# A graph network kernel: the order of three small things

## What is computed

```
h = max(layernorm(x), 0);  x = x + attention_and_splines(h)
h = max(layernorm(x), 0);  x = x + three_convolutions(h)

attention_and_splines:
  e = leaky_relu(s[row] + t[col]);  ex = exp(e - max over the row's edges)
  agg = sum(ex * h[col]) / sum(ex)                  # per node
  out = silu(agg) @ base_w.T + einsum(cubic B-splines of agg (8 per feature), spline_w)
three_convolutions, l = 0, 1, 2:
  agg = (normalised adjacency with self loops) @ (x @ W[l].T) + b[l]
  x = relu(gamma[l] * batchnorm(agg) + beta[l])
```

## Time and profile before

| what | us |
|---|---|
| median of 3 runs (614.23 to 615.87) | 615.74 |
| the profiled execution | 615.99 |
| its span, first to last instruction | 614.2 |
| PE busy | 588.1 (96%) |
| DVE busy | 435.3 (71%) |
| ACT busy | 338.8 (55%) |
| POOL busy | 36.2 (6%) |

### The profile page before, as it was taken

The page is one execution under the profiler, slowest core; times in us unless marked ns, Lnnn a source line. Parts: engine busy times, 40 slices in busy tenths (PEclk is TensorE's granted clock), DMA queues, the critical chain, the costliest instruction groups (busy, mean ns, idle before and its releaser), DMA issues.

```text
span 614.2 us, 9800 instructions
## 1 busy us (share of the span) xinstructions
PE 588.1 (96%) x3951; PEld 364.3 (59%) x3951; DVE 435.3 (71%) x745; ACT 338.8 (55%) x447; POOL 36.2 (6%) x40
## 2 busy tenths in 40 slices
PE   6798989999999999999999999999999999999994
PEld 2566856565645555555555555687557855587552
DVE  7995999987669999995499779362374335552555
ACT  3897647767799989892798334044132333142112
POOL 1000430000000000000000030041100020000000
PEclk9899799899999999999999999999999999999999
DMA  8980400000410000000000000250200000000112
GB/s 301 316 282 29 189 1 2 1 2 1 162 75 1 0 2 1 1 1 1 0 2 1 0 1 2 68 214 1 68 2 0 1 1 0 2 2 0 43 43 83
DMA packets 11502, 29.18 MB, mean 48 GB/s; under 512 B 735, under 2 KB 2399, under 8 KB 11201
## 3 DMA queue, kind: packets, MB, share of 16 engines
q1 hardware_dynamic: 11456, 28.54, 12.7%
HBM read 22.71 MB, written 5.84 MB: 46 GB/s over the span
## 4 chain that ended last, share of the span: by engine, by line
PE 68%; DVE 2%; ACT 0%; DVEq 0%; issue 0%; ACTq 0%
PE bank L1892 33%; PE bank L1976 21%; PE bank L1933 13%; DVE BHL L1306 1%; PE bank L1876 0%; PE bank L1870 0%; ACT Z L977 0%; DVE lnx L1444 0%; DVE BHL L1312 0%; DVE lnp L1442 0%; DVEq L1443 0%; DVE kx L1274 0%; DVE kh L1295 0%; DVE Z L1547 0%; ACTq L126 0%
## 5 line engine op out<-in xcount | busy, mean ns | idle before, releaser
L1892 PE MATMUL bank<-BHL,WKh 128*128 128x418 f16 x1152 | 204.5, 339 | 1.2 <-DVE BHL L1306 1.2
L1892 PEld LDWEIGHTS bank<-BHL,WKh 128*128 128x128 f16 x1152 | 111.2, 97 | 94.2 <-DVE BHL L1306 1.6
L1976 PE MATMUL bank<-C,YH 128*128 128x418 f16 x360 | 122.4, 340 | 0.0
L1976 PE MATMUL bank<-C,YL 128*128 128x418 f16 x360 | 122.3, 340 | 0.0
L1547 DVE SCALAR_TENSOR_TENSOR Z<-bank,yback,dvb 128x418 f32<-128x418 f32 x36 | 23.4, 651 | 52.1 <-PE bank L1976 52.1
L973 ACT ACTIVATE bnc<-bnm,tiny 128x1 f32<-128x1 f32 x12 | 3.5, 294 | 92.0 <-DVE bnm L1555 92.0
L1976 PEld LDWEIGHTS bank<-C,YH 128*128 128x128 f16 x360 | 35.3, 98 | 28.8 <-issue 0.8
L1976 PEld LDWEIGHTS bank<-C,YL 128*128 128x128 f16 x360 | 35.2, 98 | 28.0
L936 ACT ACTIVATE YH<-bank,dvl 128x512 f16<-128x512 f32 x30 | 20.5, 687 | 56.6 <-PE bank L1933 56.6
L1497 DVE SCALAR_TENSOR_TENSOR YL<-bank,dvl,YH 128x512 f16<-128x512 f32 x30 | 22.0, 749 | 39.1 <-ACT YH L936 39.1
L1933 PE MATMUL bank<-GWH,XH 128*128 128x512 f32 x120 | 47.6, 396 | 0.0
(11 more groups left out here) (246 smaller groups left out, 984.3 us busy)
## 6 DMA issues: line engine op xcount, KB each, us to landing
WKf<-in_wk SPq DMA_DIRECT2D x9, 1024.0 KB, 6.6
c_scratch<-C SPq DMA_DIRECT2D x1, 3200.0 KB, 10.8
C<-c_scratch SPq DMA_DIRECT2D x1, 3200.0 KB, 10.1
GWf<-in_gwT SPq DMA_DIRECT2D x3, 1024.0 KB, 11.1
XT<-in_xT SPq DMA_DIRECT2D x1, 2500.0 KB, 8.8
outT<-Z SPq DMA_DIRECT2D x3, 625.0 KB, 3.0
Wt<-in_WT SPq DMA_DIRECT2D x1, 1024.0 KB, 8.2
hx<-in_x SPq DMA_DIRECT2D x1, 1024.0 KB
```

The source lines that it names most:

```text
L1892: ins = mm(bank[:, 4 * (g % 2) + o, 0:G], lhs, rhs, start=(u == 0 and q == 0 and i == 0), stop=(u == UNITS - 1 and q == PAIR - 1 and i == 2))
L1976: ins = mm(bank[:, u % YB, 0:G], Y[:, j, o * P:(o + 1) * P], C16[:, j, g * G:(g + 1) * G], start=(j == 0 and i == 0), stop=(j == NT - 1 an ...
```

## The change

1. In DVE's attention loop `denominators(0)` moves from n = 14 to n = 13 and `weight_scale` from 13 to 14.
2. In the spline loop turn 0's own last steps (`above`, `turn_low`, `upper`, `lower`) come right behind `spline(0)` on DVE, turn 1 counts as `fresh`, and ACT does `turn_high(0)` two operations earlier, ahead of `middle(2)`.
3. The last chunk is cut into four pieces: first columns 1000 to 1249, then three pieces of 334, 334 and 332. DVE does the first alone, scale and shift in a tensor_scalar, then maximum with 0 and addition of x in one, while ACT does the relu of the others. SP issues four stores in place of three.

```diff
+OWN = 250
+THIRD = (N - OWN + 2) // 3
-PIECES = [...] + [(DC - 1, g * G, min((g + 1) * G, N)) for g in range(NG)]
+PIECES = [(c, 0, N) for c in range(DC - 1)] + [(DC - 1, N - OWN, N)] + [
+    (DC - 1, i * THIRD, min((i + 1) * THIRD, N - OWN)) for i in range(3)]
...
-                if n == 1:
-                    turn_high(0)
                 squares_of(n, i)
...
                     clipped(n + 1)
+                if n == 0:
+                    turn_high(0)
                 if n + 2 < NG * TURNS:
                     middle(n + 2)
...
-                        if k == c:
+                        if k == c and not (last and n1 - n0 == OWN):
                             nc.scalar.activation(Z[:, c, n0:n1], Z[:, c, n0:n1], ACT.Relu, bias=bnc[:, 1, c:c + 1],
                                                  scale=bnc[:, 0, c:c + 1]).then_inc(relu_set, 1)
...
                 if n == 13:
+                    denominators(0)
+                if n == 14:
                     weight_scale()
-                if n == 14:
-                    denominators(0)
...
-                fresh = n in (0, 2 * TURNS)
+                fresh = n in (0, 1, 2 * TURNS)
...
-                elif n:
+                elif n > 1:
                     silu_low(2, 1)
...
                 spline(n, i)
+                if n == 0:
+                    above(0)
+                    turn_low(0)
+                    upper(0)
+                    lower(0)
...
-                            dve.wait_ge(relu_set, l * DC + (i + 1))
+                        if k == c and i == DC - 1:
+                            dve.wait_ge(bn_set, l * DC + (c + 1))
+                            V.tensor_scalar(Z[:, c, n0:n1], Z[:, c, n0:n1], bnc[:, 0, c:c + 1], bnc[:, 1, c:c + 1],
+                                            ALU.mult, ALU.add)
+                            dve.drain()
+                            V.scalar_tensor_tensor(Z[:, c, n0:n1], Z[:, c, n0:n1], 0.0, XT[:, c, n0:n1],
+                                                   ALU.max, ALU.add).then_inc(out_set, 1)
+                        elif k == c:
+                            dve.wait_ge(relu_set, l * DC + (i + 1 if i < DC - 1 else i))
```

More of the change, by code:

```diff
@@ L117 @@
 MEAN_BANKS = (4, 5, 0)
-PIECES = [(c, 0, N) for c in range(DC - 1)] + [(DC - 1, g * G, min((g + 1) * G, N)) for g in range(NG)]
+OWN = 250
+THIRD = (N - OWN + 2) // 3
+PIECES = [(c, 0, N) for c in range(DC - 1)] + [(DC - 1, N - OWN, N)] + [
+    (DC - 1, i * THIRD, min((i + 1) * THIRD, N - OWN)) for i in range(3)]
 VAR_BANKS = (6, 1)
```

## The result

The changed kernel takes 612.92 us (median of 20 runs, 612.68 to 614.53), the kernel before 615.78 (median of 20, 614.16 to 617.51): 2.86 us less. The ratio is 0.996 with a 95% interval of 0.9951 to 0.9969. The profiled execution took 614.23 us, 612.4 of it span.

A forecast was written before the change was run, and what follows sets the result against it. PE was taken as the bound from attention to the last convolution; 2.33 + 0.17 + 0.35 = 2.85 us off the profiled 615.99 gave 613.1, and with the median 0.25 lower, 612.9 us; eight in ten 611.0 to 614.6.

The forecast's parts named there:

- Part A: Attention, group 0: inverting weight sums before the scale removes PE's 2.3 us wait and half clock; gain 2.33 us.
- The four limits: Attention groups 0 to 2: scale hidden, then row copy, second inversion and second row copy cut 4.25 us to 2.33.
- Part B: Splines: finishing turn 0 first moves PE's 1.2 us wait to turn 1, nearly 1 us there; gain 0.17 us.
- Part C: Kernel's end: DVE alone does 250 columns, last addition 0.31 us ahead, store 0.04; gain 0.35 us.
- Stalls that add up: Rival 1: DVE is not the limit, so 4.25 + 1.2 + 0.35 = 5.8 us gained, 609.9 us; chance 0.10.
- Half clock at a new place: Rival 2: one half-clock stretch returns ahead of group 2 or at turn 1, costing 1.6 us, 614.5 us; chance 0.17.
- the slower case: Rival 3: clock falls behind each new wait from 134.5 us on; two give 616.2 us, a third 617.8; chance 0.04.
- Sums too late for DVE: Rival 4: group 0's sums come after DVE's 104.69, or scale late for group 1; gain 1.5 to 2.3; chance 0.07.

The follow-up runs named there:

- both moves above: Changed kernel with the weight split behind the second inversion and row copy, and ACT's rounding right behind the squares; 610.87 us, 0.9914 of the kernel before.
- the first part alone: Kernel before with only group 0's weight sums inverted at tile 13 and the scale at tile 14; 613.48 us, ratio 0.9958.

## Why the prediction was right, point by point

**Part A: mechanism right, size 0.3 us too small, by one assumption: that DVE's total work up to the row copy is unchanged.** The four limits came in the order forecast: scale hidden, row copy, second inversion, second row copy. Forecast was 2.33 us, measured 2.65. The difference is DVE's scale: in the earlier trace rows it takes 1.82 us from 104.69 to 106.51, with a pause of 0.44 us in it that the trace lays to issue:

```profile
105.98 0.15 DVE L1236 TENSOR_SCALAR wsi<-wsi 128x1 int32<-128x1 int32 x1 [0.44 <-issue]
```

In the changed kernel its steps follow each other every 0.23 us (108.85, 109.08) and it takes 1.44. From the inversion to the row copy DVE now needs 110.96 - 106.06 = 4.90 us (its first instruction starts 0.19 ahead of the 106.25 above) where I had 109.97 - 104.69 = 5.28. Of these 0.38 us PE got 0.34: it started group 2 at 135.58, 28.34 us behind the fixed point, where the forecast had 134.55, 28.68 behind; the rest went mostly in PE going on 0.15 us behind the copy and not 0.09. The row copy in group 1 cost PE 0.11 us and not 0.5, and the scale was ready 0.7 us ahead of group 1 and not 0.3. Why the pause is gone was not tried; it is absent in all six traces of kernels with the first part and present in all six without it.

**What the prediction had wrong is what it compared with.** It took the half clock as part of the kernel before. It was part of that one execution. Against an execution without it the first two parts are worth 498.78 - 497.66 = 1.12 us and the change 1.4, which is what the lowest times differ by (614.16 and 612.68: 1.5); against one with it 3.1. The medians lie between, 2.86 apart, and that this is my 2.85 is partly luck: a term of 0.3 too small for the executions with half clock, and a share of executions without it that I did not know of (9 of the 20 times of before lie below 615). The earlier trace rows could not have told this; only the spread of the three runs hinted at it.

**Part B: right in size and in cause.** Forecast 0.17, measured 0.16, and the wait stood where it was said, ahead of turn 1. The list gives it 1.0 us, and moving it away brought 1.24: the list counts a wait from the modelled end of the matmul before, 0.34 us behind its start, while PE would have started the next one 0.18 behind. So a wait of PE in such a list costs some 0.16 us more than it says; the last 0.07 of the 1.24 stay unexplained. Of the wait behind the 134.60 matmul above, 0.64 is listed and 135.58 - 134.78 = 0.80 lost.

**Part C: total right, two terms wrong.** Additions ended 0.29 to 0.30 ahead (forecast 0.31). The tensor_scalar took 0.41 us and not 0.29. It pushed the first addition behind it to 608.62, 0.17 us after the first relu had ended (608.45), but the second began at 609.04 and the third at 609.60, each 0.03 us behind its relu (609.01 and 609.57), so the end did not move. I took the row of 836 columns in 0.59 us, but that instruction has an immediate for its scalar. The Trainium skill ("VectorE: DVE Perf Modes", "The perf-mode tier table") has float32 tensor_scalar out of SBUF at twice the rate of tensor_tensor; the rates agree with it for either kind of scalar: 418 columns more cost 0.21 or 0.22 us above, and 0.43 by the addition's 1.02 ns a column. The fixed 0.12 us for two column scalars comes on top. The store: 166 KB landed in 1.9 us as 207 KB did, so no gain shows for which the forecast had 0.04.

**The rivals.** Stalls that add up (0.10): no, 2.65 and not 4.25 for the first part. But they were there to be had behind DVE's and ACT's order: with both moves above, 500.48 - 495.18 = 5.30 us are gone from the fixed point on, of that rival's 4.25 + 1.2 = 5.45. Half clock at a new place (0.17, and two of them as the slower case, 0.04): not in the one profile of the changed kernel, nor of the first part alone, nor with the weight split moved; waits of 0.4 to 1.2 us had full clock behind them each time. The Trainium skill's rule of the swinging clock under frequent short idles ("TensorE: Matmul & The Clock Gate", "A second HAM failure mode: psum-queue depth-cycling") is not borne out by these waits, but they are few, so they hardly test it. Sums too late for DVE (0.07): no, the inversion began without a wait.

## What to carry to other kernels

Before a stall is taken away, read what the waited-for engine and its neighbours do up to the next meeting points: here 4.25 us of stall and half clock gave 2.65, and 1.2 us gave 0.16, because another engine's queue set the next limit at the meeting points right behind; two reorderings at just those limits then gave 2.5 more. Where the matrix engine waits for some 2 us, look at several executions: here the clock behind such a wait differed between executions of one kernel, and one profile shows one throw. Compare from an event just ahead of the change, not by the span.

## What the runs showed of the hardware

- Behind one and the same wait of 2.3 us the granted clock fell to 0.50 in four of five traces (in the profile before, half rate from 109.5 to 112.9 us, 1.7 us lost) and stayed at 1.00 in the fifth; with matmuls in 2.1 us of it, it stayed in the one profile taken, and the highest time came down by 1.8 us. The waits of 0.4 to 1.2 us in groups 1 and 2 and in the splines never had half clock behind them in these traces. What makes the executions reach the fixed point at 105.77 to 107.24 us was not tried; the two latest (107.24 and 107.22) are the ones with a clock of 0.89 from 35 to 50 us, the others had 1.00 there.
- Two [128, 1] column scalars add 0.11 to 0.12 us to a float32 VectorE tensor_scalar at every length from 250 to 836 columns; one adds 0.06 at 250.
- A pause of 0.44 us in the scale's row of small VectorE instructions stood in the six traces that do the scale ahead of the inversion and in none of the six that do it behind. Its cause was not tried.
- The landing time of the last store did not depend on its size between 166 and 207 KB (1.9 us for either, one store each).
